# A graph network's symmetry test: square transposes and transfers in place of TensorE transposes

## The reference, cut to what matters

```python
Af = A.astype(float32); AfT = Af.T
state = x
for _ in range(5):
    a_in  = Af  @ (state @ in_W.T  + in_b)
    a_out = AfT @ (state @ out_W.T + out_b)
    a = concat([a_in, a_out, state])
    r = sigmoid(a @ r_W.T + r_b)
    z = sigmoid(a @ z_W.T + z_b)
    h_hat = tanh(concat([a_in, a_out, r * state]) @ h_W.T + h_b)
    state = (1 - z) * state + z * h_hat
out = tanh(state @ o1_W.T + o1_b) @ o2_W.T + o2_b
return layernorm(x + out)
```

## Time and profile before

| | us |
|---|---|
| median of 3 runs | 714.21 (712.16 to 715.25) |
| the profiled execution | 710.79 |
| its span in the trace | 708.9 |
| TensorE busy | 683.9 |
| VectorE busy | 470.6 |
| ScalarE busy | 239.1 |
| POOL busy | 45.2 |

### The profile page before, as it was taken

How to read it: one execution, slowest core, us unless ns; L and a number is a source line. 1 busy time by engine, 2 the same in 40 slices (tenths; PEclk the granted TensorE clock), 3 DMA queues, 4 the chain that set the end, 5 groups by cost and what they waited for, 6 DMA issues and landing times.

```text
span 708.9 us, 8256 instructions
## 1 busy us (share of the span) xinstructions
PE 683.9 (96%) x3168; PEld 568.0 (80%) x3168; DVE 470.6 (66%) x775; ACT 239.1 (34%) x369; POOL 45.2 (6%) x38
## 2 busy tenths in 40 slices
PE   6999999999999999999999999999999999998991
PEld 6887888888888888888888888888888888886881
DVE  4777757876475767657676854657485565758794
ACT  2755645531132143203123511413252121214553
POOL 0022022000000000000000000000000000005052
PEclk9999999999999999999999999999999999999997
DMA  8873632000000000000000000000000000030003
GB/s 281 280 229 108 191 100 95 1 1 0 1 0 1 1 1 0 0 0 0 0 0 0 0 0 0 0 0 0 0 0 1 0 1 1 0 120 0 1 1 121
DMA packets 18414, 27.26 MB, mean 38 GB/s; under 512 B 1872, under 2 KB 9424, under 8 KB 18384
## 3 DMA queue, kind: packets, MB, share of 16 engines
q1 hardware_dynamic: 16864, 26.48, 11.3%
q10 hardware_dynamic: 1520, 0.40, 0.3%
HBM read 24.78 MB, written 2.10 MB: 38 GB/s over the span
## 4 chain that ended last, share of the span: by engine, by line
PE 87%; DVE 6%; DMA 3%; ACT 2%; issue 0%; SPq 0%; ACTq 0%; DVEq 0%
PE bank L432 37%; PE bank L375 15%; PE bank L377 15%; PE bank L376 15%; PE bank L404 2%; PE bank L515 2%; DVE a L805 2%; DMA stage<-in_adj_dram 1%; DMA stateT<-in_L_gnn_out_W_dram 1%; DVE rows L786 1%; ACT a L779 1%; DVE work L868 1%; DVE a L1087 1%; PE bank L384 0%; DVE ring L786 0%
## 5 line engine op out<-in xcount | busy, mean ns | idle before, releaser
L432 PE MATMUL bank<-ring,rows 128*128 128x512 f32 x1280 | 295.5, 390 | 0.9 <-ACT ring L600 0.7
L432 PEld LDWEIGHTS bank<-ring,rows 128*128 128x128 f32 x1280 | 239.5, 188 | 51.3 <-ACT ring L600 1.6
L634 ACT ACTIVATE work<-work,bias 128x512 f32<-128x512 f32 x120 | 86.6, 724 | 286.3 <-DVE work L862 285.7
L862 DVE SCALAR_TENSOR_TENSOR work<-degree,deg_w,bank 128x512 f32<-128x512 uint16 x120 | 88.9, 744 | 109.8 <-PE bank L377 109.4
L375 PE MATMUL bank<-u_c,fold 128*128 128x512 f32 x240 | 96.6, 402 | 3.1 <-DVE work L862 3.1
L791 DVE CAST ring<-a 128x1024 fp32r<-128x1024 uint8 x128 | 87.0, 688 | 12.7 <-PE bank L432 12.7
L377 PE MATMUL bank<-u_c,fold 128*128 128x512 f32 x240 | 93.8, 391 | 0.0
L376 PE MATMUL bank<-u_c,fold 128*128 128x512 f32 x240 | 93.7, 390 | 0.0
L377 PE MATMUL bank<-st_c,own 128*128 128x512 f32 x160 | 62.4, 390 | 0.0
L375 PE MATMUL bank<-st_c,own 128*128 128x512 f32 x160 | 62.3, 390 | 0.0
L376 PE MATMUL bank<-st_c,own 128*128 128x512 f32 x160 | 62.2, 389 | 0.0
(11 more groups left out here) (120 smaller groups left out, 733.3 us busy)
## 6 DMA issues: line engine op xcount, KB each, us to landing
stage<-in_adj_dram SPq DMA_DIRECT2D x28, 512.0 KB, 5.2
work<-in_x_dram SPq DMA_DIRECT2D x1, 2048.0 KB, 16.1
a<-in_x_dram SPq DMA_DIRECT2D x1, 2048.0 KB, 8.3
a<-in_adj_dram SPq DMA_DIRECT2D x3, 512.0 KB, 11.1
out_dram<-a SPq DMA_DIRECT2D x3, 512.0 KB, 3.0
a<-in_L_gnn_r_W_dram SPq DMA_DIRECT2D x1, 768.0 KB, 6.8
a<-in_L_gnn_z_W_dram SPq DMA_DIRECT2D x1, 768.0 KB, 8.8
stateT<-in_L_gnn_h_W_dram SPq DMA_DIRECT2D x1, 768.0 KB, 10.4
```

The lines of the kernel that those rows point to most:

```text
L432: last = nc.tensor.matmul(u_bank[2 * (c % 2) + d][:, :], rows[:, part, j, d * P:(d + 1) * P], ring[:, p % RING, jj, :], start=(j == 0 and ...
L634: nc.scalar.activation(gates[:, g, e, :], gates[:, g, e, :], ACT.Tanh if g == H else ACT.Sigmoid, bias=bias[:, g, e:e + 1]).then_inc(gate_ ...
L862: nc.vector.scalar_tensor_tensor(out=gates[:, g, e, :], in0=degree[:, c * CW:(c + 1) * CW], scalar=deg_w[:, g, e:e + 1], in1=g_bank[s % 3] ...
```

## The change

- **TensorE** loses `check_turn`: 8 times 4 transposes, and its waits.
- **VectorE** loses `check_expand` (8 casts). It gets `turn_squares(n)`, n = 0 to 3: one `transpose` of 128 x 1024 bytes, which transposes each 32x32 square of bytes within its group of 32 partitions, from the packed rows (which are read with a stride, 32 bytes out of each 128) into `turned_u8`. They go to the four slots of chunk 2 of step 3, behind the last pack.
- **SP** gets 16 transfers. Transfer (n, r) moves the squares of partition group r, 1024 bytes on each of 32 partitions, to partition group n, into the place of the packed rows. SP waits for all four transposes first. They stand ahead of its wait for the last expanded pair.
- **VectorE's `check(n)`** now reads the moved bytes and the packed columns, both bytes in SBUF, for n = 0 to 7. They go to the slots of chunks 1 and 2 of step 4 in place of gate chunks 0 and 1. The first waits for all 16 transfers.

```diff
--- before.py
+++ after.py
@@ -139,13 +139,20 @@
         PACK = 8
         NPK = NB // PACK
         N_PACKS = 2 * NPK * (PACK - 1)
+        FIRST_CHECK = (LAST - 1) * (NC - 1) * 2 * DB
         flat_stage = stage[:, :, :, :].rearrange("p s a w -> p (s a w)")
         pack_rows = flat_stage[:, 0:NPK * N // 4].bitcast(U32).rearrange("p (g w) -> p g w", g=NPK)
         pack_cols = flat_stage[:, NPK * N // 4:2 * NPK * N // 4].bitcast(U32).rearrange("p (b g w) -> p b g w", b=NB, g=NPK)
         rows_u8 = flat_stage[:, 0:NPK * N // 4].bitcast(U8).rearrange("p (g c w) -> p g c w", g=NPK, c=NC)
         cols_u8 = flat_stage[:, NPK * N // 4:2 * NPK * N // 4].bitcast(U8).rearrange("p (b g w) -> p b g w", b=NB, g=NPK)
         scratch = deg_sum[:, 0:CW // 4].bitcast(U8)
-        pack_f = flat_stage[:, 2 * NPK * N // 4:2 * NPK * N // 4 + 2 * CW].bitcast(F32).rearrange("p (n w) -> p n w", n=2)
+        SQ, NQ = 32, P // 32
+        blocks_u8 = flat_stage[:, 0:NPK * N // 4].bitcast(U8).rearrange("p (m c d) -> p c m d", c=NQ, d=SQ)
+        turned_u8 = flat_stage[:, 2 * NPK * N // 4:3 * NPK * N // 4].bitcast(U8).rearrange("p (c m d) -> p c m d", c=NQ, d=SQ)
+        moved_u8 = flat_stage[:, 0:NPK * N // 4].bitcast(U8).rearrange("p (r g b d) -> p r g b d", r=NQ, g=NPK, d=SQ)
 
 
         y = a8[:, 0:2, :, :].rearrange("p c b w -> p (c b w)").bitcast(F32).rearrange("p (b d) -> p b d", d=D)
@@ -179,7 +186,8 @@
         deg_part_ready = sem("f_deg_part_ready")
         degree_done = sem("f_degree_done")
         packed = sem("f_packed")
-        pack_f_ready = sem("f_pack_f_ready")
+        squares_turned = sem("f_squares_turned")
+        squares_moved = sem("f_squares_moved")
         fin_hi = sem("f_fin_hi")
         fin_lo = sem("f_fin_lo")
         zeroed = sem("f_zeroed")
@@ -195,7 +203,6 @@
         pair_stored = sem("f_pair_stored")
         pair_ready = sem("f_pair_ready")
         pair_used = sem("f_pair_used")
-        check_done = sem("f_check_done")
         check_read = sem("f_check_read")
         degree_read = sem("f_degree_read")
         agg_done = sem("f_agg_done")
@@ -290,6 +297,11 @@
                         sp.wait_ge(pair_stored, before + 1)
                     sp.dma_start(staged[slot], adj_v[:, 2 * p:2 * p + 2, c * CW:(c + 1) * CW]).then_inc(stage_loaded[slot], 16)
 
+            for n in range(NQ):
+                sp.wait_ge(squares_turned, NQ)
+                for r in range(NQ):
+                    sp.dma_start(moved_u8[n * SQ:(n + 1) * SQ, r], turned_u8[r * SQ:(r + 1) * SQ, n].rearrange("p (g b) d -> p g b d", g=NPK))\
+                      .then_inc(squares_moved, 16)
             sp.wait_ge(pair_ready, N_STEPS * S_PAIR)
             sp.dma_start(x_res, x_v).then_inc(xr_loaded, 16)
 
@@ -375,14 +387,6 @@
                 nc.tensor.matmul(out_, wh, vh, start=first, stop=False)
                 nc.tensor.matmul(out_, wh, vl, start=False, stop=False)
                 return nc.tensor.matmul(out_, wl, vh, start=False, stop=last)
-
-            def check_turn(n):
-
-                pe.wait_ge(pack_f_ready, n + 1)
-                wait(pe, check_read, n)
-                for b in range(BC):
-                    last = nc.tensor.transpose(t_bank[:, b * P:(b + 1) * P], pack_f[:, n % 2, b * P:(b + 1) * P], ident[:, :])
-                last.then_inc(check_done, 1)
 
             def degrees(c):
 
@@ -450,8 +454,6 @@
                     own_part(g_bank[s % 3], g, e, st_c)
                     if (c, s) in T_AT and not last_step:
                         turn(t, *T_AT[c, s], first)
-                    if last_step and c < NPK:
-                        check_turn(c * NC + s)
                     if last_step and (c, s) == (NPK, 1):
                         count_odd()
                     if s == 0:
@@ -820,19 +822,22 @@
                 nc.vector.scalar_tensor_tensor(out=acc, in0=first if k == PACK - 2 else acc, scalar=1, in1=block,
                                                op0=ALU.logical_shift_left, op1=ALU.bitwise_or).then_inc(packed, 1)
 
-            def check_expand(n):
-
-                wait(dve, check_done, n - 1)
-                nc.vector.tensor_copy(pack_f[:, n % 2, :], rows_u8[:, n // NC, n % NC, :]).then_inc(pack_f_ready, 1)
+            def turn_squares(n):
+
+                if n == 0:
+                    dve.wait_ge(packed, N_PACKS)
+                nc.vector.transpose(turned_u8[:, n], blocks_u8[:, n]).then_inc(squares_turned, 1)
 
             def check(n):
 
-                dve.wait_ge(check_done, n + 1)
+                if n == 0:
+                    dve.wait_ge(squares_moved, 16 * NQ * NQ)
 
                 wait(dve, check_read, n)
+                g, r = n // NQ, n % NQ
                 nc.vector.scalar_tensor_tensor(
-                    out=scratch.rearrange("p (b q) -> p b q", b=BC), in0=t_bank[:, :].rearrange("p (b q) -> p b q", b=BC),
-                    scalar=1.0, in1=cols_u8[:, n % NC * BC:(n % NC + 1) * BC, n // NC, :],
+                    out=scratch.rearrange("p (b d) -> p b d", d=SQ), in0=moved_u8[:, r, g], scalar=1.0,
+                    in1=cols_u8[:, :, g, r * SQ:(r + 1) * SQ],
                     op0=ALU.mult, op1=ALU.not_equal, accum_out=differ[:, n:n + 1]).then_inc(check_read, 1)
 
             def pair(t, c, p, first):
@@ -909,14 +914,6 @@
                     if last and (c, s) == (NC - 1, 0):
                         split_hidden(0)
 
-                def last_check(s):
-
-                    if last and c < NPK:
-                        n = c * NC + s
-                        check(n)
-                        if n + 2 < NPK * NC:
-                            check_expand(n + 2)
-
                 if first:
                     dve.wait_ge(degree_done, c + 1)
                     nc.vector.tensor_copy(degree[:, c * CW:(c + 1) * CW], t_bank[:, :]).then_inc(degree_read, 1)
@@ -924,13 +921,11 @@
                 if c == NC - 1:
                     update(t, c - 1)
                 turned(0)
-                last_check(0)
                 gate(t, c, 0)
                 final(0)
                 next_pair(0)
                 rs(t, c, 0)
                 turned(1)
-                last_check(1)
                 gate(t, c, 1)
                 rs_low(t, c, 0)
                 rs(t, c, 1)
@@ -938,14 +933,12 @@
                 next_pair(1)
                 if last and c == NPK:
                     odd_flag()
-                last_check(2)
                 gate(t, c, 2)
                 turned(2)
                 rs_low(t, c, 1)
                 final(2)
                 next_pair(2)
                 turned(3)
-                last_check(3)
                 gate(t, c, 3)
                 next_pair(3)
                 if c == NC - 2:
@@ -971,6 +964,10 @@
                         if i == 0:
                             dve.wait_ge(pair_stored, S_PAIR)
                         pack(i)
+                    elif 0 <= i - N_PACKS < NQ:
+                        turn_squares(i - N_PACKS)
+                    elif 0 <= i - FIRST_CHECK < NPK * NC:
+                        check(i - FIRST_CHECK)
 
             def step(t, first=False, last=False):
                 if first:
@@ -989,10 +986,6 @@
                     for p in range(LEAD):
                         expand(t, 1, p)
                 aggregate(t, 1, first)
-                if last:
-                    dve.wait_ge(packed, N_PACKS)
-                    check_expand(0)
-                    check_expand(1)
                 for c in range(NC):
                     gate_chunk(t, c, first, last)
                     if last and c == NPK - 1:
```

## The result

The changed kernel takes 711.15 us (median of 11 runs, 709.14 to 712.38) where the kernel before takes 713.13 (11 runs beside them, 712.16 to 715.25). The ratio is 0.997, with a 95% interval from 0.9958 to 0.9982: 2.0 us faster, between 1.3 and 3.0. That lies in the range that was given, but it is only half of the 3.7 us that were forecast. The profiled execution took 711.03 us, span 709.0, against 710.79 and 708.9 before; by the two profiles alone nothing was won. That pair flatters the kernel before: its profiled execution was faster than all but one of the 77 timed runs of that kernel on record (710.49 to 716.55). The question is where the saving went.

A forecast was written before the change was run, and what follows sets the result against it. TensorE was taken as the bound, busy for 96% of the span; -3.78 us for the removed check turns and +0.1 for a transpose stall gave -3.7, so 714.21 became 710.5 us, range 708.5 to 714.0.

The forecast's parts named there:

- What TensorE loses: Gate chunks 0 and 1 of step 4 lose the check turns: 1.89 us each, 3.78 us in all.
- The square transposes: Four VectorE transposes in the aggregate of chunk 2, step 3: 1.14 us each, against slack of 1.12 us per transpose.
- The stall: TensorE waiting for pair 7's cast in chunk 2's aggregate, step 3: 0.05 us, rounded up to 0.1.
- Rivals A and B: Square byte transposes in step 3: A 2.28 us each, 713.9 us, chance 0.08; B 4.56 us, 720.7 us, chance 0.05.
- The comparisons: Eight VectorE comparisons moved into the aggregates of chunks 1 and 2, step 4: 0.69 us each, covered, cost 0.
- The transfers: SP's 16 transfers of 32 KB from about 472 us, ending near 500, ahead of their use: cost 0.
- Rival C: SP's moves land one behind another, late for step 4's comparisons: at 6 us each +3.6, 717.8 us, chance 0.03.
- Rival D: Turns leave TensorE, but step 4's chunks 0 and 1 stay at 18.2 us: 714.2 us, chance 0.02.
- the sentence on POOL's additions: Late in the span, POOL's four residual additions and TensorE's 3.05 us wait move with the last cast: no net change.
- The sign that had been named: In the changed profile, TensorE's late wait for VectorE was to stay near 3 us.
- about 2 us to either side: Spread given to the likeliest case, since a landing 1 us off changes the overlap at POOL's late additions.

The follow-up runs named there:

- experiment 1: Kernel before and changed kernel, each with POOL's four additions left out (709.09, 704.12 us), or with x loaded in three parts and POOL held (709.14, 703.91 us).
- the one with 17 matmuls: Changed kernel with POOL's additions held until ScalarE's first sigmoid of gate chunk 2, step 4, and 17 unread matmuls in TensorE's wait: 708.98 us, ratio 0.9934.
- the kernel with the hold: Changed kernel with POOL's additions held until ScalarE's first sigmoid of gate chunk 2 of step 4: 710.97 us, ratio 0.997.

## Why the prediction was right in sign and range and half wrong in size

- **What TensorE loses: right.** 3.78 us by the earlier trace rows; 1.88 and 1.89 measured.
- **The square transposes: right.** The groups by line in the changed kernel (busy us, mean ns, idle before):

```profile
L838 DVE SCALAR_TENSOR_TENSOR deg_sum<-stage 128x512 uint8<-128x512 uint8 x8 | 5.5, 684 | 0.0
L829 DVE STREAM_TRANSPOSE stage<-stage 128x1024 uint8<-128x1024 uint8 x4 | 4.9, 1233 | 0.0
```

VectorE's timeline at the first of them:

```profile
464.29 1.23 DVE L829 STREAM_TRANSPOSE stage<-stage 128x1024 uint8<-128x1024 uint8 x1
465.45 0.65 DVE L793 CAST ring<-a 128x1024 fp32r<-128x1024 uint8 x1
```

  1.233 us busy and 1.16 from start to start, the pace of the other rows of 1024 elements, for bytes too. 1.14 had been taken from the rows; the estimate from the Trainium skill, "VectorE: DVE Perf Modes", section "The three transpose paths", was 1.16. The stall was 0.02 us for 0.1; the cast behind a transpose shows 0.65 busy instead of 0.69, which gave a little back. Rivals A and B fell with this row.
- **The comparisons: right.** 684 ns each, no idle time before the first, and the aggregates keep 14.50 and 14.51 us.
- **The transfers: right.** 16 issues from 472.5 to 482.5 us, 1.9 us to landing each, 75 us ahead of their use. Rival C had no case.
- **Rival D: out**, the chunks did shrink to 16.3 us.
- **The step that failed** is the sentence on POOL's additions: "Everything in it moves with the last cast, so I expect no net change." The issue of the load did move with the last cast. Its landing did not, because an instruction transfer of TensorE's program, whose place hangs on the number of instructions and not on the cast, came to lie in it. The sign that had been named, a late wait still near 3 us, failed with it. That 1.2 us came back as a wait 1.17 us longer and, in the profile, 2.44 us of half clock. In the earlier trace rows I had seen the wait and taken it for scatter "about 2 us to either side"; that margin is why the range held. Part of the nearness to 710.5 is luck as well: the kernel before came out at 713.13 over 11 runs where the forecast stood on 714.21 from three, which hid 1.1 us of the 1.7 us by which the saving fell short. The later landing was systematic, and there were places to look for it: how long the load takes, what else is in the DMA view around it, and whether the change moves that.
- **The accounting.** In the profiles: -3.77 + 0.02 + 3.61 + 0.9 (start, scatter) and -0.6 behind the last products, together +0.1 against the measured +0.1. In the timed runs -2.0, and -2.3 when the changed kernel was timed again. With the longer wait alone the sum would be -3.75 + 1.17 = -2.6. The clock's part can be estimated from the mean granted clock that is on record for each timed run: on average 0.9913 in 26 runs of the kernels in which that wait is gone or filled (experiment 1 and the one with 17 matmuls), 0.9892 in 66 runs of the kernel before, 0.9877 in 23 of the changed kernel. So the kernel before seems to fall to the lower level there in part of its runs too, though its profile, at 0.993, did not; no single run's mean says where in the span it fell, and the stretch behind TensorE's last product counts in it too, so this is rough. The difference of 0.0015 is 1.1 us of lost clock over 711 us. In the changed profile 6.8 us at half clock, 3.4 us lost, cost 2.44 us; at that rate 1.1 us cost an estimated 0.8, and the sum is -1.8. On average the half clock thus costs the changed kernel something like 1 us more than the kernel before, not 2.4 us.

## What to carry to other kernels

An edit that removes instructions moves that engine's instruction transfers against everything else; where a load is on a tight path, look for an instruction packet in its stretch before and after. A wait on the bounding engine that is already in the profile is not neutral ground: ask what starts it, whether that moves with the change, and what the clock does behind it. And when a saving vanishes, lay all stretches of both traces side by side first. Here one table named the only stretch that had changed, and taking its cause away (x loaded in parts, POOL where VectorE is idle) was worth more than the change itself (3.9 us in the kernel before, 7.2 us in the changed one, by the medians).

## What the hardware showed that I had not expected

- A 2 MB load lands 1.2 us later (9.2 to 9.7 us in seven profiles instead of 8.2 to 8.3 in four) when one 16 KB instruction transfer falls beside its 2064 packets.
- VectorE's products of two SBUF operands take 2.77 and 2.88 us instead of 0.69 beside POOL's additions, while its degree additions, with one operand in PSUM, keep 0.75. The Trainium skill, "SBUF — State Buffer", section "Who interferes with whom", says that a VectorE instruction with two SBUF inputs contends with a GpSimd instruction that reads SBUF, and one with at most one SBUF input, outside the 2-port modes, does not. The trace agrees.
- Filling a wait of TensorE with useless matmuls made the kernel with the hold 2.0 us faster (710.97 to 708.98 us); in its profile the clock in that chunk then stayed at the upper level.
